# A GNN layer on one core: sixteen places for node tiles in PSUM, and the compared lane numbers in SBUF

## What is computed

```
h       = relu(layernorm(x))
msg     = relu(h[src] + edge_attr)                     # 25000 x 256
p       = msg @ W_fc.T + b_fc                          # 25000 x 256
scores  = p @ Q.T                                      # four heads
alpha   = softmax of scores over the edges of one dst
gate    = softmax(mean of p over the edges of one dst @ Wg.T + bg)
predict = sigmoid(sum over heads and edges of gate * alpha * p)
out     = x + predict                                  # 50000 x 256
```

## Time and profile before

| | us |
|---|---|
| median of 3 runs | 739.03 (735.18 to 739.16) |
| profiled execution | 734.6 |
| its span on the core | 732.9 |
| edge stage | 0 to about 350 |
| weights | about 350 to 400 |
| node stage | 400 to the end |

### The profile page before, as it was taken

The page is one execution under the profiler, slowest core; times in us unless marked ns, Lnnn a source line. Parts: engine busy times, 40 slices in busy tenths (PEclk is TensorE's granted clock), DMA queues, the critical chain, the costliest instruction groups (busy, mean ns, idle before and its releaser), DMA issues.

```text
span 732.9 us, 12416 instructions
## 1 busy us (share of the span) xinstructions
PE 548.9 (75%) x2474; PEld 434.1 (59%) x2475; DVE 487.6 (67%) x1644; ACT 383.3 (52%) x661; POOL 453.4 (62%) x339
## 2 busy tenths in 40 slices
PE   2417988878779868879403998888888778877785
PEld 2205876666558656758202876776667566665564
DVE  4208678788879768769798766666565655555555
ACT  2105455656457545647211254666666666666674
POOL 7765565665560656550053366777877887778785
PEclk9999899999999999989855999999999999999999
DMA  7434455555553468775300799999999999999999
GB/s 223 131 93 134 147 173 174 165 174 154 174 170 114 129 224 271 237 234 191 115 0 1 247 355 383 314 307 329 357 319 329 325 327 339 325 337 336 341 333 332
DMA packets 137238, 171.53 MB, mean 234 GB/s; under 512 B 10096, under 2 KB 123784, under 8 KB 137202
## 3 DMA queue, kind: packets, MB, share of 16 engines
q10 hardware_dynamic: 91344, 90.23, 37.6%
q1 hardware_dynamic: 33010, 42.70, 18.6%
q0 software_dynamic: 12848, 38.20, 16.5%
HBM read 111.50 MB, written 59.60 MB: 233 GB/s over the span
## 4 chain that ended last, share of the span: by engine, by line
PE 52%; issue 12%; ACT 11%; DVE 10%; another core or an unknown queue 5%; ACTq 4%; DVEq 3%; POOL 2%; DMA 2%; POOLq 0%; SPq 0%
PE bank L745 24%; PE bank L829 18%; PE bank L735 7%; ACT arena L597 5%; DVE spread L1248 3%; ACT bank L573 3%; POOL arena L478 2%; ACTq L600 2%; DVEq L1252 1%; ACT arena L505 1%; ACTq L552 1%; ACTq L605 1%; ACT arena L497 1%; DMA p_keep<-p_spill 1%
## 5 line engine op out<-in xcount | busy, mean ns | idle before, releaser
L829 PE MATMUL bank<-p_keep,spread 128*128 x1172 | 274.1, 388 | 51.6 <-DVE spread L1248 46.7
L829 PEld LDWEIGHTS bank<-p_keep,spread 128*128 128x128 f32 x1172 | 219.0, 192 | 107.5 <-issue 79.8
L1248 DVE TENSOR_SCALAR spread<-bank,rel,wgt 128x128 f32<-128x128 f32 x586 | 195.8, 404 | 128.5 <-PE bank L829 72.8
L478 POOL TENSOR_TENSOR arena<-arena 128x1024 f32<-128x1024 f32 x96 | 224.9, 2352 | 73.1 <-ACT arena L597 72.7
L745 PE MATMUL bank<-w_all,arena 128*128 128x264 f32 (+1 forms) x784 | 228.0, 417 | 53.2 <-ACT arena L505 40.2
L745 PEld LDWEIGHTS bank<-w_all,arena 128*128 128x128 f32 (+1 forms) x784 | 143.7, 204 | 78.9 <-ACT arena L505 50.9
L597 ACT ACTIVATE arena<-bank 128x1024 f32<-128x1024 f32 x97 | 99.2, 1023 | 139.3 <-PE bank L829 120.3
L443 POOL DMA_INDIRECT p_keep<-in_x_dram,idx x124 | 120.8, 975 | 72.6 <-issue 31.5
L505 ACT ACTIVATE arena<-bank 128x256 f32<-128x256 f32 x196 | 73.6, 376 | 124.2 <-PE bank L735 71.0
L443 POOL DMA_INDIRECT arena<-in_x_dram,idx x72 | 70.1, 973 | 64.7 <-ACT arena L497 33.7
L573 ACT ACTIVATE bank<-zero 128x1024 f32<-128x1024 f32 x98 | 100.5, 1026 | 3.0
(11 more groups left out here) (202 smaller groups left out, 190.6 us busy)
## 6 DMA issues: line engine op xcount, KB each, us to landing
out_dram<-arena ACTq DMA_DIRECT2D x97, 512.0 KB, 4.5
arena<-in_x_dram ACTq DMA_DIRECT2D x73, 512.0 KB, 5.4
arena<-in_edge_attr_dram SPq DMA_DIRECT2D x48, 512.0 KB
arena<-in_x_dram POOLq DMA_DIRECT2D x24, 512.0 KB, 5.8
p_spill<-p_keep SPq DMA_DIRECT2D x16, 512.0 KB
p_keep<-p_spill SPq DMA_DIRECT2D x16, 512.0 KB, 5.8
p_keep<-in_x_dram,idx POOLq DMA_INDIRECT x124
arena<-in_x_dram,idx POOLq DMA_INDIRECT x72
```

The costliest lines, as they stand in the source:

```text
L478: pool.tensor_tensor(yout[:, slot, :, :], yout[:, slot, :, :], xin[:, slot, :, :], ALU.add).then_inc(summed, 1)
L829: nc.tensor.matmul(places[:, bass.ds(place, T)], spread[:, k0 + k, :], p_rows[:, bass.ds(p_at, T)], start=False, stop=True, skip_group_che ...
L1248: v.tensor_scalar(spread[:, k, :], bank[:, 7, P:2 * P], rel[:, bass.ds(s0 + k, 1)], wgt[:, bass.ds(s0 + k, 1)], ALU.is_equal, ALU.mult).th ...
```

## The change

- POS becomes 16 and SLOTS 4: four groups are in flight in all 8 banks. The table's division by the number of places is now a multiplication by 512 where it was 683.
- Bank 7 is no longer free for the lane numbers. They are written to `lane`, a tile of 128 x 128 float32 in SBUF, and every spread reads them there.
- Three of the four slots are cleared where the three were before. The fourth (banks 6 and 7) is cleared after DVE has copied the weights of both parts out of these banks. DVE raises `wgt_ready` a second time for this.

```diff
-    POS = 12
+    POS = 16
...
-    assert all((j * 683) >> 13 == j // POS for j in range(NODES))
+    assert all((j * 512) >> 13 == j // POS for j in range(NODES))
...
+        lane = sb("lane", [P, P])
...
-            for z in range(SLOTS):
+            for z in range(SLOTS - 1):
                 clear(z)
             act.wait_ge(words_in, 64)
-            act.wait_ge(wgt_ready, 1)
+            act.wait_ge(wgt_ready, 2)
+            clear(SLOTS - 1)
...
-                    v.tensor_scalar(place_nj, node_nj, 683.0, None, ALU.mult).then_inc(table_step, 1)
+                    v.tensor_scalar(place_nj, node_nj, 512.0, None, ALU.mult).then_inc(table_step, 1)
...
-                    v.tensor_scalar(bank[:, 7, P:2 * P], column[:, :], dst_0, None, ALU.subtract).then_inc(node_step, 1)
+                    v.tensor_scalar(lane[:, :], column[:, :], dst_0, None, ALU.subtract).then_inc(node_step, 1)
...
-                    v.tensor_scalar(spread[:, k, :], bank[:, 7, P:2 * P], rel[:, bass.ds(s0 + k, 1)],
+                    v.tensor_scalar(spread[:, k, :], lane[:, :], rel[:, bass.ds(s0 + k, 1)],
                                     wgt[:, bass.ds(s0 + k, 1)], ALU.is_equal, ALU.mult).then_inc(spread_ready, 1)
...
             then(v.tensor_copy(wgt[:, P:STEPS], bank[:, 6, 0:STEPS - P]))
+            dve.sem_inc(wgt_ready, 1)
```

## The result

The changed kernel takes 806.14 us (median, 804.25 to 807.86), the kernel before 739.1 on the same chip: a ratio of 1.092 (95% interval 1.087 to 1.097), slower by 67 us. The forecast was 799.

A forecast was written before the change was run, and what follows sets the result against it. No single bound before, a ring of engines; then spreads and POOL additions excluding each other. Additions 216.4, spreads 128.5 and idle 9 made 354 us for 295; +60 in all, 739 + 60 = 799 us, own range 765 to 835, wider 750 to 860.

The forecast's parts named there:

- The exclusion: Node stage: each DVE spread reading SBUF two columns at a time and each POOL addition exclude each other; forecast chance 0.64.
- The bridge to a one-source spread: Node stage: exclusion seen for two SBUF inputs also holds for the one-input spread; L1201 took 0.66 us beside POOL.
- The spread alone: DVE in the node stage: from SBUF a spread takes 0.33 us, pitch 0.25 us, bounds 0.19 and 0.32.
- The sum: 430 to 725 us: additions 216.4, spreads 128.5, neither working 9; together 354 us instead of 295, +59 us.
- the time in which neither works: Node stage, POOL and DVE both idle: 0.1 us a group, 9 us; bounds -0.1 and 0.56 a group.
- Sixteen places: Node stage: DVE's 49.9 us of waiting for clears goes, but another limit was expected to take its place first.
- rival 1: Node stage: no exclusion, so the kernel gets faster by 20 to 30 us, to 714 us; chance 0.11.
- Rival 2: Node stage: no exclusion, and the transfers are the bound at 337 GB/s, so no change, 739 us; chance 0.05.
- POOL's own loads: Node stage: POOL's own transfers, 23 x 0.77 us, lie beside spreads and add nothing.
- Two of the signs to look for: Node stage: spreads up to 2.7 us when an addition runs; additions up to 4 us behind a batch of spreads.
- rival 4: Node stage: POOL gets in after every spread, DVE's lead is lost; 5.2 us a group, 840 us, up to 920; chance 0.12.
- PE's clock: Node stage: a fall from more rest could double PE's 244 us; given no chance of its own.

## Why the prediction was right

- **The exclusion is shown.** It appears with the two-column mode (1.10), goes without it at the same source (0.987), and goes when the additions go (0.958). The prediction had it from rows on instructions with two sources. The bridge to a one-source spread rested on one row, L1201, and proved right, but the row doesn't carry it. L1201 ended at 381.84, while POOL's instruction beside it ran on for another 1.0 us, so it had not waited for that one:

```profile
381.08 1.76 POOL L458 TENSOR_SCALAR logits<-step_tile,tile_f 128x586 f32<-128x586 f32 x1
```

- **The spread alone** was put at 0.33 us and a pitch of 0.25. It took 0.335, and six of them 1.63 us: a pitch of (1.63 - 0.335) / 5 = 0.26.
- **The sum**, 354 us for the window of 295, came out as 368. With the pitch and the duration measured, additions are 92 x 2.366 = 217.7 us and spreads 517 x 0.26 = 134.4, which leaves 16 us as a remainder. Counted from the starts and ends of the instructions the parts are others: some addition ran for 215 us, a spread outside the additions for 124, and neither for 29. A stopped spread needs less than a pitch after its release (it ends 0.08 us later in the median). So the mis-sized term is the time in which neither works: 9 us were taken, 0.1 a group, and it was 29, or 0.32, still under the bound of 0.56. That the sum came out 14 us short and not 20 is luck: the additions' term was 1 too large and the spreads' 5.
- **Sixteen places** were to stop DVE's waiting for clears and bring nothing. Both hold under the exclusion. Without it they leave 28.0 to 38.6 us of that wait and bring 1%, less than the 3% of rival 1 (714 us).
- **Rival 2**, that the transfers are the bound, was wrong: the versions with fewer additions move 366 GB/s. It may be the next limit (385 GB/s in the best slices), but it is not this one.
- **POOL's own loads** were put at nothing, beside the spreads. That was wrong: each can stop a spread and hand it on to the additions behind it, and all 20 stops over 2.7 us came about in this way. What they cost is not known.
- **Two of the signs to look for were wrong.** I expected an addition of up to 4 us behind a batch of spreads and a spread of at most 2.7. POOL was never held for long (2.49 us at most) and DVE for up to 5.43. POOL gets in behind the spread that is running, as rival 4 had it. That didn't cost what rival 4 said. The likely reason, argued and not shown, is that POOL then runs dry (118 us of waiting for sigmoids), and in that time DVE catches up.
- **PE's clock** was given no chance, and it fell: 0.89 in the window, 0.99 before. PE's busy time is 274 us instead of the 245 foreseen. The stretches around the stop shown above (PE, then granted clock, DMA share, GB/s):

```profile
646.00:648.00 2.00, 1.91 (x8) 1.00 0.93 264
648.00:650.00 2.00, 0.05 (x1) 1.00 0.86 249
650.00:652.00 2.00, 0.00 (x0) 0.88 1.04 364
652.00:654.00 2.00, 1.90 (x5) 0.50 1.00 344
654.00:656.00 2.00, 2.00 (x9) 0.77 0.23 80
```

PE rests for 4 us, and the clock goes from the upper level (2.4 GHz) to the lower one (1.2 GHz) at about the time when work comes again: 5 matmuls in 2 us instead of 8 to 11. What this adds to the 806 us stays open. By PE's own account the stage's 73 us are 30 us of longer matmuls and 43 us of more idle time. By that of DVE and POOL they are the lost overlap. DVE waited for PE less than before (50 us, it was 67), so PE's slower stretches can hardly cost more than the 29 us in which neither DVE nor POOL worked. That is argued, not shown; no run held the clock up.

## What to carry to other kernels

Before a DVE operand moves from PSUM to SBUF, look at what GpSimd does at that time. A one-source float32 instruction that becomes faster by the move (404 to 335 ns here) also begins to exclude GpSimd's instructions. Add up both engines' times for one turn of the loop. Near what the slowest other engine needs, the exclusion cost next to nothing here (a sum of 2.7 us beside PE's 2.65). A sum of 3.8 us made turns of 4.0 (368 / 92) where they had been 3.2, and the whole kernel 9 to 10% slower. Transfers that GpSimd issues belong to its side as well: they start the longest stops. If PSUM is wanted for something else, keep the operand in SBUF and give source and destination outermost counts that keep the instruction at one column a time: this gave the gain of the sixteen places (1%) without the loss.

## What the runs showed of the hardware

- The exclusion is one-sided here: 96 additions of 2.34 to 2.49 us, spreads of up to 5.43. All 20 spreads over 2.7 us began during a load that POOL issues.
- Splitting the addition in two lets DVE finish one spread between the halves (stops of 1.3 us), except behind a load (up to 5.72 us).
- A load issued on GpSimd, 0.77 us, stops the two-column spread too (up to 0.60 us, with nothing else on POOL).
- A memset on GpSimd, which reads nothing, stops the two-column spread too (468 ns in the mean instead of 348).
- A tensor in SBUF read as 3 rows of 44 and written as one run of 132 takes 402 ns, the duration of 128 columns from PSUM (404), and isn't disturbed.
- After 4 us without work PE's clock stood at the lower level for the next 2 us of work.
